# Last expert stage of a two-layer language-model tower as a pipeline over batches, with regions, a row table and ten pairs in flight

## What is computed

```python
logits = (flat @ router_w).astype(jnp.float32) + router_bias      # 16 experts
probs = jax.nn.softmax(logits, axis=-1)
top_w, top_i = jax.lax.top_k(probs, TOPK)                         # 2 a token
norm_w = top_w / (jnp.sum(top_w, axis=-1, keepdims=True) + 1e-06)
...
routed = combine[:, E - 1:E] * flat                               # expert 15 is the identity
for e in range(E - 1):
    y = jax.nn.silu(flat @ expert_gate_w[e]) * (flat @ expert_up_w[e]) @ expert_down_w[e]
    routed = routed + combine[:, e:e + 1] * y
...
gate = conv_general_dilated(x_ncw, conv_w, window_strides=(1,), padding=[(KS - 1, 0)], ...)
shared = jax.nn.silu(gate) * (hidden_states @ shared_up_w) @ shared_down_w
return shared + routed
```

## Time and profile before

| | us |
|---|---|
| median of 3 runs | 2643.86 |
| lowest, highest | 2642.42, 2650.0 |
| profiled execution | 2641.9 |
| span of its profile | 2640.2 |
| mean granted clock of TensorE over it | 0.907 |

### The profile page before, as it was taken

One profiled execution on the slowest core, in us unless ns is written; L12 is line 12 of the kernel. 1 busy time (PEld: TensorE's weight loads), 2 busy tenths in 40 slices (PEclk: granted clock), 3 DMA queues, 4 the chain that ended last, 5 costly groups with the idle time before them and its releaser, 6 DMA issues. The chain is left out here.

```text
span 2640.2 us, 43175 instructions
## 1 busy us (share of the span) xinstructions
PE 2182.8 (83%) x13073; PEld 1686.4 (64%) x13073; DVE 1586.9 (60%) x4474; ACT 1325.2 (50%) x2652; POOL 744.7 (28%) x835
## 2 busy tenths in 40 slices
PE   3899999999999999767882873888888989695982
PEld 2788888887888888635662651555555556463772
DVE  4555665565556656356764977767777768541225
ACT  2344544454445444345545763867776768210330
POOL 5111111111111111042446662122212222226442
PEclk8899999999999999989986985988989989678996
DMA  5620010000000000022232535222122221303446
GB/s 108 166 33 0 11 33 1 8 13 24 1 8 3 1 1 0 27 65 51 43 64 68 147 109 177 78 67 64 49 70 74 71 69 51 101 33 108 127 137 243
DMA packets 209472, 165.36 MB, mean 63 GB/s; under 512 B 108320, under 2 KB 167376, under 8 KB 209296
## 3 DMA queue, kind: packets, MB, share of 16 engines
q1 hardware_dynamic: 190832, 120.71, 17.3%
q0 software_dynamic: 14240, 38.35, 4.6%
q10 hardware_dynamic: 4224, 4.19, 0.5%
HBM read 91.07 MB, written 72.11 MB: 62 GB/s over the span
## 5 line engine op out<-in xcount | busy, mean ns | idle before, releaser
L630 PE MATMUL psum_o<-w_s,hid_s 128*128 128x256 f32 x3072 | 384.0, 284 | 19.1 <-ACT hid L434 19.1
L616 PE MATMUL psum_h<-xn2T_s,w_s 128*128 128x512 f32 x1536 | 389.9, 404 | 5.4 <-ACT hid L434 3.6
L630 PEld LDWEIGHTS psum_o<-w_s,hid_s 128*128 128x128 f32 x3072 | 371.8, 188 | 27.0 <-issue 19.1
L433 ACT ACTIVATE hid_s<-psum_h,b 128x512 fp32r<-128x512 f32 x256 | 176.5, 689 | 391.5 <-PE psum_h L616 376.0
L616 PEld LDWEIGHTS psum_h<-xn2T_s,w_s 128*128 128x128 f32 x1536 | 283.5, 191 | 87.1 <-ACT hid L434 21.8
L2126 DVE CUSTOM_DVE_ANT_0 ra_z<-ra_psum_s,rhat 128x128 f32<-128x128 f32 (+3 forms) x512 | 224.9, 483 | 132.6 <-PE ra_psum_s L2234 120.5
L2076 ACT ACTIVATE ra_z<-ra_z,ra_nm 128x128 f32<-128x128 f32 (+3 forms) x512 | 245.4, 563 | 0.0
L2007 POOL TENSOR_SCALAR_AFFINE_SELECT ra_z<-ra_z 128x512 f32<-128x512 f32 x128 | 81.6, 637 | 477.3 <-DVE ra_z L2157 477.3
L2246 PE MATMUL ra_psum_p<-ident,ra_z 128*128 128x128 f32 x1280 | 181.4, 293 | 1.3 <-ACT turned L2068 1.3
L517 DVE TENSOR_TENSOR hid_s<-hid,hid_s 128x1024 fp32r<-128x1024 f32 x128 | 156.0, 1223 | 43.1 <-ACT hid L434 42.1
L2068 ACT ACTIVATE turned<-ra_psum_p 128x1024 f32<-128x1024 f32 x128 | 131.3, 1026 | 92.1 <-PE ra_psum_p L2246 92.1
(11 more groups left out here) (380 smaller groups left out, 4212.4 us busy)
## 6 DMA issues: line engine op xcount, KB each, us to landing
ex_slots<-blank SPq DMA_DIRECT2D x1, 10296.0 KB, 33.8
ex_zT<-ex_slots SPq DMA_DIRECT2D x39, 264.0 KB, 3.0
ex_rows<-ex_slots SPq DMA_DIRECT2D x8, 1056.0 KB, 9.3
w<-in_L_tok_w SPq DMA_DIRECT2D x8, 1024.0 KB, 7.5
ra_scratch<-ra_hi SPq DMA_DIRECT2D x32, 256.0 KB
ra_scratch<-ra_lo SPq DMA_DIRECT2D x32, 256.0 KB
ra_q_st<-ra_scratch SPq DMA_DIRECT2D x128, 64.0 KB, 1.8
ra_k_st<-ra_scratch SPq DMA_DIRECT2D x128, 64.0 KB, 1.8
```

Source lines behind the costliest of these rows:

```text
L433: act.activation(hid_s[:, 0, m, :], psum_h[:, m % 2, :], ACT.Gelu, bias=b1[:, m:m + 1])
L616: mm = pe.matmul(psum_h[:, m % 2, :], w1_s[:, w_part, k, m * P:(m + 1) * P], xn2T_s[:, x_part, k, :], start=(n == 0 and k == 0), stop=(n = ...
L630: mm = pe.matmul(psum_o[:, t // 2, (t % 2) * D:(t % 2 + 1) * D], hid_s[:, h_part, m, t * P:(t + 1) * P], w2_s[:, w_part, m, :], start=(n = ...
```

## The change

Routing goes batch by batch. Each of the 15 routed experts owns a fixed region of 8 * 512 + 128 rows in `ex_slots`, so the slots of a batch are known when this batch is counted (`used` holds the next free slot of each expert). A blank block is written behind the last row of each region (15 writes of 128 rows, half by SP, half by ACT). The pair loop reads the first row of each block from a table in SBUF, with one transfer and one register read for each block instead of one for each pair, and `RING` and `YRING` become 10 and 8. The second copy of a token goes from a copy of the rows, `rows1`, which ACT makes (two batches deep). The maxima are found with `max` and `max_index`. The shared expert of batch b - 3 (`LAG`) is issued behind the routing of batch b, and its inputs have one PSUM bank each instead of two. The shares of the two experts are worked out at the end.

```diff
+        self.ex_region = NB * T + P
+        self.ex_dummy = self.ex_experts * self.ex_region
...
-        RING, YRING = 6, 4
+        RING, YRING = 10, 8
@@ SP
-            for c in range(2):
-                sp.wait_ge(sent[c], 16 * NT)
+            sp.wait_ge(pads_made, 2)
+            sp.wait_ge(pad_ready, 1)
+            for e in range(0, EX, 2):
+                at = sp.value_load(pad_at[0:1, e:e + 1], min_val=0, max_val=DUMMY - P)
+                sp.dma_start(slots[ds(at, P), :], pads[:, e, :]).then_inc(pad_stored, 16)
+            sp.wait_ge(S.ex_cleared, 16)
+            sp.wait_ge(table_ready, 2)
             sp.wait_ge(gu_done, NB)
+            sp.wait_ge(pad_stored, 16 * EX)
+            sp.wait_ge(sent, 16 * NT)
+            for n in range(2):
+                sp.wait_ge(sent1[n], 8 * NT)
             for j in range(PAIRS):
...
-                sp.dma_start(zs[:, j % RING, :, :], slots[2 * j * P:(2 * j + 2) * P, :].rearrange("(s p) c -> p s c", p=P)).then_inc(zs_loaded[j % RING], 16)
+                for s in range(2):
+                    at = sp.value_load(row_at[0:1, 2 * j + s:2 * j + s + 1], min_val=0, max_val=DUMMY + (BLOCKS - 1) * P)
+                    sp.dma_start(zs[:, j % RING, s, :], slots[ds(at, P), :]).then_inc(zs_loaded[j % RING], 16)
@@ POOL
+            def scatter(b):
+                pool.wait_ge(slot_ready, b + 1)
+                for n in range(b * TT, (b + 1) * TT):
+                    pool.indirect_dma_start(slots, bass.IndirectOffsetOnAxis(ap=slot[:, 0, n:n + 1], axis=0),
+                                            rows[:, n, :], None).then_inc(sent, 16)
+                if b >= 2:
+                    pool.wait_ge(sent1[b % 2], 16 * TT * (b // 2))
+                pool.iota(rows1[:, b % 2, :, D].bitcast(I32), ...).then_inc(marked, 1)
+                pool.wait_ge(marked, b + 1)
+                pool.wait_ge(copied, b + 1)
+                for t in range(TT):
+                    pool.indirect_dma_start(slots, bass.IndirectOffsetOnAxis(ap=slot[:, 1, b * TT + t:b * TT + t + 1], axis=0),
+                                            rows1[:, b % 2, t, :], None).then_inc(sent1[b % 2], 16)
...
             for b in range(NB):
+                if b + 2 < NB:
+                    rstd_of(b + 2)
+                scatter(b)
@@ ACT
+            for b in range(NB):
+                turned(b)
+                copy_rows(b)
+                if b >= LAG:
+                    silu(b - LAG)
+            act.wait_ge(pads_made, 2)
+            act.wait_ge(pad_ready, 1)
+            for e in range(1, EX, 2):
+                at = act.value_load(pad_at[0:1, e:e + 1], min_val=0, max_val=DUMMY - P)
+                act.dma_start(slots[ds(at, P), :], pads[:, e, :]).then_inc(pad_stored, 16)
+            for b in range(NB - LAG, NB):
+                silu(b)
+            act.wait_ge(soft_in, 2)
+            act.activation(other[:, :, :], other[:, :, :], ACT.Exp)
+            act.activation(second[:, :], gap[:, :], ACT.Exp, scale=-1.0).then_inc(soft_out, 1)
@@ DVE
+            norm_stats(0)
+            norm_apply(0)
+            norm_stats(1)
+            prepare()
+            norm_apply(1)
+            for i in range(NB):
+                if i >= 1:
+                    settle(i - 1)
+                if i + 2 < NB:
+                    norm_stats(i + 2)
+                if i + 2 < NB:
+                    norm_apply(i + 2)
+                choose(i)
+                if i >= LAG:
+                    hidden(i - LAG)
+                if i >= LAG + 1:
+                    add_shared(i - LAG - 1)
+            settle(NB - 1)
+            table()
+            soft()
+            hidden(NB - LAG)
+            add_shared(NB - LAG - 1)
+            for b in range(NB - LAG + 1, NB):
+                hidden(b)
+                add_shared(b - 1)
+            shares()
+            add_shared(NB - 1)
@@ PE
+            turn(0)
+            prepare()
+            router(0)
+            for b in range(1, NB):
+                turn(b)
+                count(b - 1)
+                router(b)
+                if b >= LAG:
+                    shared_gate(b - LAG)
+                    shared_up(b - LAG)
+                if b >= LAG + 1:
+                    shared_down(b - LAG - 1)
+            count(NB - 1)
+            for b in range(NB - LAG, NB):
+                shared_gate(b)
+                shared_up(b)
+                shared_down(b - 1)
+            shared_down(NB - 1)
```

More of the change, by code:

```diff
@@ L2293, in experts_stage @@
     DOWN = 2 * DK * I
-    NEVER = -3.0e38
     with ExitStack() as ctx:
@@ L2457, in _ @@
             act.activation(second[:, :], gap[:, :], ACT.Exp, scale=-1.0).then_inc(soft_out, 1)
-            for b in range(NB):
-                silu(b)
             for i in range(PAIRS + 2):
@@ L2516, in norm_apply @@
                 last.then_inc(z_ready, 1)
-            norm_stats(0)
-            for b in range(NB):
-                if b + 1 < NB:
-                    norm_stats(b + 1)
-                norm_apply(b)
-            dve.wait_ge(consts_made, 2)
-            dve.tensor_copy(descend[:, :], iota_i[:, :])
-            dve.tensor_copy(step[:, :], step_i[:, :])
-            dve.tensor_copy(place[:, :], place_i[:, :])
-            dve.tensor_copy(block[:, :], block_i[:, :]).then_inc(consts_cast, 1)
-            dve.wait_ge(consts_cast, 1)
@@ new lines, in choose @@
+            def choose(b):
+                group = slice(b * TT, (b + 1) * TT)
+                dve.wait_ge(logits_done, b + 1)
+                dve.tensor_tensor(logits[:, group, :], bank[6][:, 0:TT * E].rearrange("p (t e) -> p t e", t=TT),
+                                  rb[:, :].unsqueeze(1).to_broadcast([P, TT, E]), ALU.add).then_inc(logits_taken, 1)
+                dve.wait_ge(logits_taken, b + 1)
+                for t in range(TT):
+                    last = dve.max(top8[:, t, :], logits[:, b * TT + t, :])
+                link(last)
+                for t in range(TT):
+                    last = dve.max_index(top_i[:, t, :], top8[:, t, :], logits[:, b * TT + t, :])
+                dve.tensor_copy(best[:, :, group], top8[:, :, 0:2].rearrange("p t c -> p c t"))
+                link(last)
+                link(dve.tensor_copy(pick[:, :, :], top_i[:, :, 0:2]))
+                for c in range(2):
+                    last = dve.tensor_tensor(hot[:, c, :, :], lane[:, :].unsqueeze(1).to_broadcast([P, TT, E]),
+                                             pick[:, :, c:c + 1].to_broadcast([P, TT, E]), ALU.is_equal)
+                link(last)
+                dve.tensor_tensor(chosen[:, :, :], hot[:, 0, :, :], hot[:, 1, :, :], ALU.add).then_inc(chosen_ready, 1)
@@ new lines, in soft, with shares @@
+            def soft():
+                dve.tensor_tensor(other[:, :, :], logits[:, :, :], best[:, 0, :].unsqueeze(2).to_broadcast([P, NT, E]), ALU.subtract).then_inc(soft_in, 1)
+                dve.tensor_tensor(gap[:, :], best[:, 0, :], best[:, 1, :], ALU.subtract).then_inc(soft_in, 1)
+            def shares():
+                dve.wait_ge(soft_out, 1)
+                link(dve.tensor_reduce(total[:, :], other[:, :, :], AX_X, ALU.add))
+                link(dve.tensor_scalar(den[:, :], total[:, :], 1e-6, 1.0, ALU.mult, ALU.add))
+                link(dve.tensor_tensor(den[:, :], den[:, :], second[:, :], ALU.add))
+                link(dve.reciprocal(share[:, 0, :], den[:, :]))
+                link(dve.tensor_tensor(share[:, 1, :], share[:, 0, :], second[:, :], ALU.mult))
@@ L2600, in _ @@
-            hidden(1)
-            dve.wait_ge(soft_out, 1)
-            link(dve.tensor_reduce(total[:, :], other[:, :, :], AX_X, ALU.add))
-            link(dve.tensor_scalar(den[:, :], total[:, :], 1e-6, 1.0, ALU.mult, ALU.add))
-            link(dve.tensor_tensor(den[:, :], den[:, :], second[:, :], ALU.add))
-            link(dve.reciprocal(share[:, 0, :], den[:, :]))
-            link(dve.tensor_tensor(share[:, 1, :], share[:, 0, :], second[:, :], ALU.mult))
-            for b in range(NB):
-                if b >= 2:
-                    hidden(b)
-                add_shared(b)
+            norm_stats(0)
@@ L2665, in router, with count @@
                                        start=(k == 0), stop=(k == DK - 1))
                 mm.then_inc(logits_done, 1)
-            turn(0)
-            pe.wait_ge(prep_copied, 1)
-            for b in range(NB):
-                if b + 1 < NB:
-                    turn(b + 1)
-                router(b)
-            def shared_first(b):
+            def count(b):
+                if b == 0:
+                    pe.wait_ge(consts_made, 2)
+                else:
+                    pe.wait_ge(counts_taken, b)
+                pe.wait_ge(chosen_ready, b + 1)
+                each = bank[7][:, 0:2 * TT * E].rearrange("p (w e t) -> p w e t", w=2, e=E)
+                by_expert = chosen[:, :, :].rearrange("p t e -> p e t")
+                pe.matmul(each[:, 0, :, :], ones[:, :], by_expert, start=True, stop=True)
```

(1 more changed line is left out.)

257 lines of the change are left out of this document (130 added, 127 removed).

## The result

The changed kernel took 2641.89 us (median of 20 executions, 2636.05 to 2646.9), the kernel before 2647.34 (20 executions, 2639.73 to 2654.86): ratio 0.9978, 95% interval 0.997 to 0.9987. So it is faster by 5.5 us (3.4 to 8 by the interval), where 11.6 were forecast: 0.22%, less than the 0.3% from which the prediction calls a kernel faster. The profiled execution took 2636.05 us with a span of 2634.1 (before 2641.9 and 2640.2).

The account below looks back on a forecast made before the run. POOL's scatters were taken to bound the routing, and the ring of six the pair loop at 3.9 us a pair. Loop start +12.1 and loop -23.7 gave -11.6 us: 2631.3 us forecast, range 2618 to 2648.

Parts of the forecast that it names:

- the sum: Whole last stage: loop start 12.1 us later plus pair loop 23.7 us shorter, together -11.6 us.
- From batch 6 on PE sets the pace: Last routing turns: PE bounds them; slots of batch 6 at 2406.2, after a turn without a pause batch 7 at 2417.6.
- Low level only partly over in each of the last four bursts: +0 to +8: PE's shared expert work: possible extra us from the lower clock level, listed beside the forecast's total.
- The pair loop: Loop over pairs: with a ring of 10, 3.25 us a pair instead of 3.9, so -23.7 us.
- A batch: Routing of batches 3 to 7: DVE and POOL in series, 18 us a batch, POOL scattering in ten.
- The tail: Shared expert of batches 5 to 7: PE idles 5.4 us before gate 6; pair loop starts at 2453.9, 12.1 later.
- Rival B: Shared expert: PE stays at 1.2 GHz, costing 45 us, time 2676; chance 0.10.
- The last rival: Routing: DVE not held by POOL, a batch every 12 us, loop some 35 us earlier, near 2596; chance 0.02.

Follow-up runs that it names:

- run 1: The kernel before with only the ring sizes raised from 6 and 4 to 10 and 8; 2624.29 us against 2645.92, ratio 0.9909.
- run 2: The changed kernel with six pairs of input in flight instead of ten, eight of results kept; 2685.1 us, ratio 1.0144 to the kernel before.
- run 3: The changed kernel with the power of a batch asked for one turn earlier, ahead of POOL's scatters; 2608.04 us, ratio 0.9857 to the kernel before.
- run 4: The changed kernel with all blank blocks written by SP and hidden product and addition ahead of the table on DVE; 2636.51 us, ratio 0.9956.
- run 10: The changed kernel, unchanged, on the second chip; 2676.72 us, ratio 0.9879 to the kernel before on that chip.
- run 14: The changed kernel, unchanged, once more on a chip of the first kind; single time 2624.0 us, stage 354.6 us.
- run 8: The changed kernel with power one turn ahead, late memset, LAG = 1 and blank blocks ten by SP, five by ACT; 2630.28 us, ratio 0.9743.
- run 7: The changed kernel with power one turn ahead, the reordered tail and the late memset, lag three, second chip; 2638.94 us, ratio 0.9755.
- run 6: The changed kernel with POOL's memset and marking moved ahead of the last batch's scatters, second chip; 2669.73 us against 2703.47, ratio 0.9877.
- run 9: The kernel before, unchanged, on the second chip; 2710.46 us, stage 388.0 us.

## Why the prediction was right or wrong

**What kept the gain under the forecast.** By the stage, which leaves out what was not changed, the change is worth 9.5 us (364.4 before, the mean of four, 354.9 after), and the sum said 11.6: 2.1 too much. The medians differ by 5.5 us (3.4 to 8 by the interval). The four us between 9.5 and 5.5 are not placed: the profiled starts of the changed kernel's stage are no later than those of the other, and one start varies by more than this. In each of runs 1 to 4, too, the medians gain 1 to 4 us less than the stages, and run 1 differs from the kernel before by its rings alone, so the gap does not belong to the new routing.

**The step that failed** is "From batch 6 on PE sets the pace. [...] The next turn without a pause: router 1.7, 6.9". The mechanism was right and the size of this term was not. Times behind the first statistics (forecast from 2278.2), in three traces of the changed kernel:

| us | forecast | result | run 10 | run 14 |
|---|---|---|---|---|
| slots of batch 5 | 113.9 | 113.7 | 113.8 | 113.8 |
| slots of batch 6 | 128.0 | 127.5 | 127.7 | 127.8 |
| slots of batch 7 | 139.4 | 141.9 | 144.1 | 143.8 |
| start of the loop | 175.7 | 179.6 | 180.7 | 180.4 |

The turn forecast at 11.4 us took 14.4 in the result's trace, 16.4 and 16.1 in the others. In the result's trace gate and up took 8.6 us instead of 6.9, since part of the gate ran at the lower level, and transposes and counts, between the down and the router, took 2.2 instead of 1.1, since PE waited 0.95 us for ACT's copy: there was a pause. The gate took 7.09 there, 8.33 in run 10 and 8.27 in run 14. One more us came at the gate and up of batch 6: 10.0 instead of 9. The prediction had five us at half the clock from the earlier trace rows, which cost 2.5 and make 9.4 of 6.9, not 9. So the loop started 3.9 us late; 1.1 came back in it (134.0 instead of 135.1), the end added 0.3, which leaves the stretch from the first statistics at 353.5 instead of 350.4. The prediction had this case beside the sum ("Low level only partly over in each of the last four bursts: +0 to +8") and took zero.

**The pair loop: right.** -24.8 against -23.7, and -23.7 with the rings alone. Of its working, "15.77 us for 14" are 1.13 us each; the 1.15 is that of the eight writes. Nothing hangs on it.

**A batch: right.** 17.7 us against 18; a turn with product and addition 18.8 against 19.5. The slots of batch 5 came at 113.7 us where 113.9 were forecast. Two errors met in this number: the memset's 2.4 us, which I had not seen though it stands in the diff, and cycles taken 0.3 to 0.7 too long; that they cancel is luck. Run 3 shows what the series of the two engines cost: 32 us.

**The tail: right in kind.** The pause of 5.30 us, both its causes at 2432 (ACT's writes to 2431.97, DVE's `table` and `soft` to 2431.7), the table load and the 1.5 us ahead of the loop are there. No row stood behind the 1.5, PE's two register reads; it was measured as 1.47 from the end of the last addition. Run 4 took away the pause ahead of the gate of batch 6, left 2.25 us ahead of the next, and won 4 us.

**Rival B** (PE stays low in the shared part) did not come: behind 2340 the clock is 0.80. But its mechanism made some 2.7 of the 3.9 us, the wait for ACT's copy one more. A gate takes 5.31 us at the higher level and took 6.8 to 8.4 in the turns of the changed kernel in which PE had waited. The Trainium skill says so (TensorE: Matmul & The Clock Gate, HAM oscillation): waits that recur make pieces start cold. The trace agrees in kind and not in full. In runs 3 and 8 gates of 5.40 us, all at the higher level, stand behind waits of 1 us, and behind the same wait of 2.25 us ahead of the last gate run 4 has 7.11 us and run 7 5.42. What decides between them was not found.

**The last rival** ("DVE not held by POOL", loop 35 us earlier) became the experiment: with power ahead the loop starts 32 us earlier.

**On the second chip** the same change is worth 34 us (0.9879); by the stages 24 of them are what the stage of the kernel before is longer there, and its traces show the standstill in it. Nothing in the rows of the first chip could have told of it. That the standstill has to do with the unbroken scatters was only argued.

## What to carry to other kernels

When a change has several parts, price them alone: here one line (the rings) was worth 24 us, and the pipeline that came with it cost 15 of them, because an operation of 1 us on POOL was queued behind the ten us of scatters that the same turn released. In a pipeline over batches ask of each small operation on the queue of a slow one whether its input was ready a turn earlier, and issue it there. And where PE waits in each turn, even for a us, a gate that takes 5.3 us without a pause is to be priced as a range, here 5.4 to 8.4, and not at its best.

The best version by the stage, run 8, took 2630.28 us on the second chip, 0.9743 of the kernel before; its stage is 41 us shorter than the changed kernel's. On the first chip the best measured was run 3 with 2608.04.

## What the hardware showed that was not expected

- DVE's small casts between buffers in SBUF were held to the end of a POOL memset that had begun 0.9 us ahead of them (2.75 us instead of 0.16; gone in run 6), its copies from PSUM were not. The Trainium skill (SBUF — State Buffer, SBUF: two separate sides) has the two engines share a pair of ports which one holds for a whole instruction; the trace agrees.
- In the lap of run 2, SP needs 1.91 us from the landing that frees a place to the start of the pair's second transfer (2489.85 to 2491.76).
- One program took 57 to 64 us longer on two other chips (2646 against 2703 and 2710). On one of them, in run 9, the last stage of the kernel before began some 35 us later (2317.9 against 2276.6 to 2288.5), and was itself 24 us longer, with signals of PE that came up to 39 us behind the work, DVE standing still for 42 us and PE for 29.
